# Attention outputs moved by DMA instead of transposes, context tiles turned beside the value projection, and the two maxima pairs of a step placed apart

## The chip, the cores and the metric

The kernel runs on one core of one Trainium2 chip, in one launch for the whole batch. The metric is the device time in microseconds; the kernel before took 1804.34 us (median of three runs, 1802.04 to 1804.83).

## The reference, cut to what matters

Eight batch elements, each with 512 query rows and 1601 context rows of 256 columns, go through cross attention (16 heads of 16 columns) and then a feed-forward part whose four linear layers' operands are rounded to FP4 in blocks of 16.

```python
q = split(layernorm(x) @ Wq.T + bq); k = split(ctx @ Wk.T + bk); v = split(ctx @ Wv.T + bv)
attn = softmax(einsum('bhqd,bhkd->bhqk', q, k) / 4)
x = x + merge(einsum('bhqk,bhkd->bhqd', attn, v)) @ Wo.T + bo
h = silu(fp4(layernorm(x)) @ fp4(w_gate).T) * (fp4(layernorm(x)) @ fp4(w_up).T)
out = x + fp4(h) @ fp4(w_down).T
```

## The kernel before, in words

**Steps.** A batch element's attention is 52 steps: 4 groups of 4 heads, and in each group 13 tiles of the context (`KROWS`: twelve of 128 rows and one of 65). In step n PE makes the scores of two heads (`scores(n, 0)`, line 685, tile `st`), does a large job, makes the scores of the other two heads (`scores(n, 1)`, the same two banks of `st`), makes products for the maxima (`pair_products`, line 699, tile `mx`), does a small job, and multiplies the probabilities of the step before with the values (`weighted`, line 714, tile `pvb`). ACT takes the exponentials (`exps`, line 870) out of `st` into `prob`; the second pair of scores can go to a bank of `st` only when the first pair's exponential has been read out of it.

**Maxima.** The row maxima that the softmax subtracts are made ahead, from bf16 leading parts of q and k, 104 products per batch element, two in each step. A product fills two banks of `mx`, with two heads at once on two halves of the array's rows (48 rows from row 0 and 48 from row 64). DVE reduces each (line 941, 1024 columns) and frees its banks. Before the change both products of a step stand behind the second pair of scores, and in the first batch element a third one behind line 714 for ten steps.

**Jobs.** All other PE work is spread over the steps by a table written by hand: `SLOTS[n]` names the jobs of side 0 (the large one) and of side 1 (the small one), each as (kind, index, part). A part says whose batch element it is: "att" the current one, "early" the next one's projections, "late" the feed-forward of the one before, "once" the weights' rounding, "next" one further ahead. Kinds: `ctxT` turns the context rows (two tiles of 128 per job, line 559), `xnT` the normed queries and `xqT` the FP4 rows (line 521), `k`, `q`, `v` the projections (lines 582, 570, 589), `gate`, `up`, `down0`, `down` the feed-forward (lines 632, 644, 652), `hqT` its rounded middle (line 640), `nm` the maxima (line 597). All of them use one PSUM bank, `misc`, so a job waits until ACT or DVE has taken the one before. `DVE_EXTRA` and `POOL_WORK` are the same kind of table for work on DVE and POOL, placed behind the maxima and the takings of a step.

**Attention's way out, before.** A group's output and the sums of its weights (a 17th column of ones in `vv`) stand in `pvb` as columns by queries. ACT copies them to `pvs` (line 876), PE turns them (`pvT`, line 601, four transposes), ACT copies values and sums apart (lines 811, 812), DVE divides (`group_divided`, lines 999 and 1002), and two jobs `attT` turn the finished rows back (line 521) for the output projection `o` (line 611).

**Iterations.** The program is unrolled: "pre" (projections of the first element), "first", six "loop", "last", and "tail" (the last element's feed-forward). SP issues nearly all DMAs in one order written by hand (`body` of the sync block), each behind its waits: keys and queries go out to memory in three bf16 parts and come back stacked for the scores.

## Time and profile before

| | |
|---|---|
| runs, median of 3 | 1804.34 us |
| the profiled execution | 1801.16 us, span 1799.4 us, granted clock 0.984 |
| PE busy | 1687.2 us, 94% |
| DVE, ACT, POOL busy | 1398.6, 1155.4, 528.4 us (78%, 64%, 29%) |
| chain that ended last | PE 74%, DVE 15%, ACT 7% |
| one batch element in the loop | 210.3 us, 52 steps |

The slices of the page show PE at 9 tenths of every slice from the second to the 36th, with the clock at full; before that the first projections wait for memory, and after it the tail's feed-forward alternates between PE and DVE. PE's matmuls are pipelined: the time that one takes from the engine is the distance between its start and the next one's start, and not its listed length.

### The profile page before, as it was taken

What the parts mean: (1) busy time and instruction counts of PE and PEld (TensorE: products, weight loads), DVE (VectorE), ACT (ScalarE), POOL (GpSimd) and SP (SyncE); (2) the same over time, 40 slices, a digit from 0 to 9 for tenths busy, and PEclk for the clock granted to TensorE, in tenths of its full rate; (3) what the DMA queues carried; (4) which work ended last, traced back from release to release, by engine and by line L of the source; (5) the groups of instructions that cost most, each with busy time, mean ns of one, the idle gap of its engine ahead of it and who ended that gap; (6) DMA issues with size and microseconds to landing.
All of it is one profiled execution on the core that took longest, in us unless ns stands there. A gap on an engine that the chain in (4) does not pass through costs nothing.

```text
span 1799.4 us, 26659 instructions
## 1 busy us (share of the span) xinstructions
PE 1687.2 (94%) x9600; PEld 658.4 (37%) x9600; DVE 1398.6 (78%) x1969; ACT 1155.4 (64%) x2335; POOL 528.4 (29%) x409
## 2 busy tenths in 40 slices
PE   3799789999999999999999999999999999989978
PEld 2332124333343343433443333433334334423425
DVE  6777887888868887788878888688877887688538
ACT  2366567776667666776667766676667766666651
POOL 4316340442107320152204421073201622012213
PEclk8899999999999999999999999999999999999989
DMA  6643432142323322043221423243220422300000
GB/s 147 151 77 92 90 77 37 47 116 38 55 37 96 91 49 50 13 110 73 55 52 44 118 40 55 37 96 90 50 48 12 108 40 43 52 1 1 7 18 12
DMA packets 98031, 109.09 MB, mean 61 GB/s; under 512 B 18788, under 2 KB 83308, under 8 KB 97900
## 3 DMA queue, kind: packets, MB, share of 16 engines
q1 hardware_dynamic: 93344, 103.26, 27.1%
q10 hardware_dynamic: 4556, 4.13, 1.1%
q8 instruction: 76, 1.25, 0.3%
q14 instruction: 55, 0.45, 0.1%
HBM read 76.78 MB, written 30.16 MB: 59 GB/s over the span
## 4 chain that ended last, share of the span: by engine, by line
PE 74%; DVE 15%; ACT 7%; issue 3%; DMA 1%; ACTq 0%; POOL 0%; SPq 0%; DVEq 0%; POOLq 0%
PE pvb L714 19%; PE st L685 18%; PE mx L699 9%; PE misc L632 7%; DVE cmx L941 6%; PE misc L582 5%; ACT prob L870 4%; PE misc L589 4%; PE misc L644 2%; PE misc L652 2%; PE misc L521 1%; PE misc L640 1%; PE misc L611 1%; PE misc L570 1%; PE misc L559 1%
## 5 line engine op out<-in xcount | busy, mean ns | idle before, releaser
L870 ACT ACTIVATE prob<-st 128x512 f32<-128x512 f32 x1630 | 887.6, 599 | 419.9 <-PE st L685 418.2
L941 DVE TENSOR_REDUCE cmx<-mx 128x2 f32<-128x1024 f32 x768 | 905.3, 1219 | 215.4 <-PE mx L699 211.7
L685 PE MATMUL st<-qstack,kstack 112*128 112x512 bf16 x1630 | 520.6, 386 | 32.6 <-ACT prob L870 20.0
L714 PE MATMUL pvb<-prob,vv 128*17 128x512 f32 (+1 forms) x3328 | 440.7, 601 | 0.6 <-ACT prob L870 0.6
L685 PEld LDWEIGHTS st<-qstack,kstack 112*128 112x128 bf16 x1630 | 128.4, 98 | 554.9 <-issue 315.7
L699 PE MATMUL mx<-kstack,qstack 48*128 48x512 bf16 (+1 forms) x2048 | 253.3, 336 | 32.8 <-DMA qstack<-scr_q 16.3
L1202 POOL TENSOR_TENSOR cin<-cin 128x400 f32<-128x400 f32 (+1 forms) x60 | 55.3, 922 | 418.6 <-ACT cin L798 418.6
L1235 POOL TENSOR_TENSOR ht<-ht,rh 128x704 f32<-128x704 f32 x29 | 40.2, 1385 | 425.0 <-DVE rh L917 425.0
L632 PE MATMUL misc<-wguT,rowsT 128*128 128x352 f32 x456 | 154.9, 462 | 0.0
L699 PEld LDWEIGHTS mx<-kstack,qstack 48*128 48x128 bf16 x2048 | 58.0, 94 | 195.7 <-issue 147.2
L632 PEld LDWEIGHTS misc<-wguT,rowsT 128*128 128x128 f32 x456 | 87.1, 191 | 41.4 <-issue 1.0
L589 PE MATMUL misc<-wv,ctxT 128*128 128x256 f32 (+1 forms) x392 | 101.9, 382 | 0.0
L714 PEld LDWEIGHTS pvb<-prob,vv 128*17 128x17 f32 (+1 forms) x3328 | 55.1, 95 | 117.4 <-issue 98.1
L582 PE MATMUL misc<-ctxT,wk 128*128 128x400 f32 (+1 forms) x240 | 91.9, 505 | 0.0
L589 PEld LDWEIGHTS misc<-wv,ctxT 128*128 128x128 f32 (+1 forms) x392 | 73.0, 187 | 21.2 <-issue 0.7
L1239 POOL TENSOR_TENSOR ht<-ht,mt 128x704 f32<-128x704 f32 x30 | 50.4, 1679 | 64.5 <-DVE mt L1120 64.5
L1206 POOL TENSOR_TENSOR cin<-cin 128x400 bf16<-128x400 f32 (+1 forms) x60 | 60.7, 1011 | 4.7
L1215 POOL TENSOR_TENSOR x<-x,bob 128x1024 f32<-128x1024 f32 x8 | 18.9, 2362 | 145.2 <-DMA x<-x 145.2
L975 DVE SCALAR_TENSOR_TENSOR ht<-misc,ht 128x352 f32<-128x352 f32 x57 | 29.7, 521 | 39.4 <-PE misc L632 39.4
L943 DVE TENSOR_REDUCE cmx<-mx 128x8 f32<-128x520 f32 x64 | 44.5, 695 | 19.3 <-PE mx L699 18.3
L1204 POOL TENSOR_TENSOR cin<-cin,one 128x400 bf16<-128x400 f32 (+1 forms) x60 | 56.4, 940 | 4.7
L582 PEld LDWEIGHTS misc<-ctxT,wk 128*128 128x128 f32 x240 | 46.1, 193 | 24.2 <-issue 1.7
(201 smaller groups left out, 1593.3 us busy)
## 6 DMA issues: line engine op xcount, KB each, us to landing
kstack<-scr_k SPq DMA_DIRECT2D x384, 100.1 KB, 4.3
scr_k<-cin SPq DMA_DIRECT2D x48, 300.0 KB, 3.2
qstack<-scr_q SPq DMA_DIRECT2D x372, 32.0 KB, 1.9
cin<-ctx_in SPq DMA_DIRECT2D x8, 1280.0 KB, 6.6
scr_q<-qp SPq DMA_DIRECT2D x15, 384.0 KB, 5.4
scr_k<-cin SPq DMA_DIRECT2D x16, 300.8 KB, 4.4
xn<-x SPq DMA_DIRECT2D x8, 512.0 KB, 3.9
x<-x SPq DMA_DIRECT2D x8, 512.0 KB, 3.8
```

Of the source, the lines that this page charges most:

```text
L582: last = mm(o[:, 0:w], wk[:, h, m * 128:(m + 1) * 128], ctxT[:, h, COFF[n]:COFF[n] + w], start=(h == 0), stop=(h == NC2 - 1))
L589: last = mm(o[0:w, 0:E], ctxT[:, h, KOFF[j]:KOFF[j] + w], wv[:, h, :], start=(h == 0), stop=(h == NC2 - 1))
L632: last = mm(o[:, 0:IH], rowsT[:, h, t * 128:(t + 1) * 128], wguT[:, h, first:first + IH], start=(h == 0), stop=(h == NC2 - 1))
L685: mm(score_bank(it, n, pair, h)[0:KROWS[kt], :], kstack[:, hd, KOFF[kt]:KOFF[kt] + KROWS[kt]], qstack[:, hd, :], start=True, stop=True).th ...
L699: last = mm(mx[:, q % 2, par, at:at + w], qstack[r0:r0 + LEAD, hd, t * 128:(t + 1) * 128], kstack[r0:r0 + LEAD, hd, k0:k0 + w], start=True ...
L714: last = mm(pvb[32 * h:32 * h + D + 1, :], vv[0:w, kt, HG * g + h, :], prob[0:w, n % 2, h, :], start=(kt == 0), stop=(kt == NKT - 1))
L870: activate(prob[0:KROWS[kt], n % 2, 2 * pair + h, :], score_bank(it, n, pair, h)[0:KROWS[kt], :], ACT.Exp, scale=SCALE).then_inc(exp_done[ ...
L941: v.tensor_reduce(cmx[:, g % 2, h0:h0 + 2, at:at + 1], products, op=ALU.max, axis=AX.X).then_inc(max_free, 1)
L1202: g_.tensor_tensor(whole, whole, parts[:, 0, :], ALU.subtract).then_inc(step, 1)
L1204: g_.tensor_tensor(parts[:, 1, :], whole, one[:, 0:1].to_broadcast([128, whole.shape[-1]]), ALU.mult).then_inc(step, 1)
L1206: g_.tensor_tensor(parts[:, 2, :], whole, parts[:, 1, :], ALU.subtract).then_inc(done, 1)
L1239: g_.tensor_tensor(y, y, m, ALU.add).then_inc(h_step, 1)
```

## The change

Four things change together. **One:** the order within a step. The first product for the maxima stands directly behind the first pair of scores, ahead of the large job, and the second one stays behind the second pair of scores; DVE's list has the first reduction ahead of the taking of the large job. **Two:** the attention's way out. `vv` holds, per pair of heads, 16 value columns, 16 ones, 16 value columns, and a head multiplies 32 neighbouring ones of these, so its sum of weights comes out 16 times. SP moves values and sums from `pvs` to `att` and `sums` by eight DMAs of 16 rows by 512 columns a group; DVE divides in eight pieces of 128 columns; `pvT`, `attT` and their copies go. **Three:** a context tile is turned right behind each `v` job (its "guest", two transposes into the other half of `misc`), instead of in seven jobs of two tiles. **Four:** jobs move up into the free slots; `xnT` uses the storage of `mt`, and some waits guard that.

```diff
 SLOTS = {
-    0: ([("v", 8, "att")], [("ctxT", 0, "early")]),
-    1: ([("v", 9, "att")], [("pvT", 3, "late")]),
-    2: ([("v", 10, "att")], [("attT", 0, "late")]),
-    3: ([("v", 11, "att")], [("attT", 1, "late")]),
-    4: ([("v", 12, "att")], [("ctxT", 1, "early")]),
-    5: ([("o", 0, "late")], [("ctxT", 2, "early")]),
-    6: ([("o", 1, "late")], [("ctxT", 3, "early")]),
-    7: ([("ctxT", 4, "early")], [("ctxT", 5, "early")]),
-    8: ([("ctxT", 6, "early")], [("xnT", 0, "early")]),
-    9: ([("k", 0, "early")], [("xnT", 1, "early")]),
+    0: ([("v", 8, "att")], [("ctx2", 0, "once")]),
...
+    4: ([("v", 12, "att")], []),
+    5: ([("o", 0, "late")], []),
+    6: ([("o", 1, "late")], []),
+    7: ([("xnT", 0, "early")], []),
+    8: ([("xnT", 1, "early")], []),
+    9: ([("k", 0, "early")], []),
...
-    18: ([("pvT", 0, "att")], [("xqT", 0, "late")]),
-    19: ([("k", 7, "early")], [("xqT", 1, "late")]),
+    18: ([("k", 7, "early")], []),
+    19: ([("xqT", 0, "late")], [("xqT", 1, "late")]),
...
-    31: ([("gate", 5, "late")], [("pvT", 1, "att")]),
+    31: ([("gate", 5, "late")], []),
...
-    41: ([("down", 2, "late")], [("pvT", 2, "att")]),
+    41: ([("down", 2, "late")], []),
...
 DVE_EXTRA = {
...
+    2: [("late", "values", 4)], 3: [("late", "values", 5)], 4: [("late", "values", 6)], 5: [("late", "values", 7), ("late", "stats", 0)], 6: [("late", "stats", 1)],
...
+    29: [("att", "values", 0)], 30: [("att", "values", 1)], 32: [("att", "values", 2)], 33: [("late", "hscale", 2)], 34: [("late", "hpower", 2)], 35: [("att", "nm", 3)], 36: [("att", "values", 3)], 39: [("late", "hscale", 3)], 40: [("late", "hpower", 3)],
...
+            def values_in(it, g, part):
+
+                sp.wait_ge(pvs_done, it.count(part, NG, g + 1))
+                c, s = divmod(g, 2)
...
+                for h in range(HG):
+                    row = HALF * s + D * h
+                    values, weights = 2 * D * h + D * (h % 2), 2 * D * h + D * (1 - h % 2)
+                    sp.dma_start(att[row:row + D, c, :], pvs[values:values + D, :]).then_inc(values_row[g], 16)
+                    if it.kind != "tail":
+                        sp.dma_start(sums[row:row + D, :], pvs[weights:weights + D, :]).then_inc(values_row[g], 16)
...
                     elif kind == "o":
+                        pe.wait_ge(att_ready, c(NC2 * QT, QT + 2 * j + 2))
...
+                def context_tile(job):
+                    _, j, part = job
...
+                    w, o = KROWS[j], job_bank(it, job)
+                    for h in range(NC2):
+                        last = turn(o[:, h * 128:h * 128 + w], ctx_rows[0:w, j, h * 128:(h + 1) * 128], ident[0:w, 0:w])
+                    last.then_inc(full["ctxT"], 1)
...
-                        last = mm(pvb[32 * h:32 * h + D + 1, :], vv[0:w, kt, HG * g + h, :], prob[0:w, n % 2, h, :], start=(kt == 0), stop=(kt == NKT - 1))
+                        last = mm(pvb[2 * D * h:2 * D * (h + 1), :], vv[0:w, kt, (HG * g + h) // 2, D * (h % 2):D * (h % 2 + 2)], prob[0:w, n % 2, h, :], start=(kt == 0), stop=(kt == NKT - 1))
...
                     if has_att:
                         scores(n, 0)
+                    products = maxima(it, n)
+                    for job in products[:1]:
+                        pair_products(job)
                     for job in jobs(it, n, 0):
                         shared(job)
                     if has_att:
                         scores(n, 1)
-                    products = maxima(it, n)
-                    for job in products[:2]:
+                    for job in products[1:2]:
                         pair_products(job)
...
+                def values_divided(part, n):
+
+                    c, t = divmod(n, QT)
+                    cols = slice(128 * t, 128 * (t + 1))
+                    if t == 0:
+                        for g in (2 * c, 2 * c + 1):
+                            dve.wait_ge(values_row[g], it.count(part, 128, 128))
+                    v.reciprocal(sums[:, cols], sums[:, cols]).then_inc(rec_ready, 1)
+                    dve.wait_ge(rec_ready, it.count(part, NC2 * QT, n + 1))
+                    v.tensor_tensor(att[:, c, cols], att[:, c, cols], sums[:, cols], ALU.mult).then_inc(att_ready, 1)
...
                 for n in range(STEPS):
+                    todo = maxima(it, n)
+                    for job in todo[:1]:
+                        maximum(job)
                     for job in jobs(it, n, 0):
                         take(job)
...
-                    for job in todo:
+                    for job in todo[1:]:
                         maximum(job)
```

In the built program, PE's list at step 2 of a loop iteration (a `v` job, line 589 before and 652 now) reads as follows, first before:

```order
L685 MATMUL st<-qstack,kstack 128x512 x2
L589 MATMUL misc<-wv,ctxT 128x256 x2
L685 MATMUL st<-qstack,kstack 128x512 x2
L699 MATMUL mx<-kstack,qstack 128x512 x4
L521 MATMUL misc<-ident,att 128x128 x4
L714 MATMUL pvb<-prob,vv 17x512 x4
```

The same step now:

```order
L751 MATMUL st<-qstack,kstack 128x512 x2
L765 MATMUL mx<-kstack,qstack 128x512 x2
L652 MATMUL misc<-wv,ctxT 128x256 x2
L728 MATMUL misc<-ident,cin 128x128 x2
L751 MATMUL st<-qstack,kstack 128x512 x2
L765 MATMUL mx<-kstack,qstack 128x512 x2
L780 MATMUL pvb<-prob,vv 32x512 x4
```

Half of the products for the maxima moved between the first scores and the projection, four transposes of `att` went, and two of a context tile came behind the projection.

DVE's list from step 2 to the two steps with the output projection, now (the pieces of the division are lines 1076 and 1078, the reductions for the maxima line 1014, the takings of `o` line 1039):

```order
L1014 TENSOR_REDUCE cmx<-mx 128x2 x3
L1076 RECIPROCAL sums<-sums 128x128
L1078 TENSOR_TENSOR att<-att,sums 128x128
L1014 TENSOR_REDUCE cmx<-mx 128x2 x2
L1076 RECIPROCAL sums<-sums 128x128
L1078 TENSOR_TENSOR att<-att,sums 128x128
L1014 TENSOR_REDUCE cmx<-mx 128x2 x2
L1076 RECIPROCAL sums<-sums 128x128
L1078 TENSOR_TENSOR att<-att,sums 128x128
L1014 TENSOR_REDUCE cmx<-mx 128x2
L1039 TENSOR_TENSOR x<-misc,x 128x512
L1014 TENSOR_REDUCE cmx<-mx 128x2
```

Before, the same stretch held one division of a group and the reductions:

```order
L941 TENSOR_REDUCE cmx<-mx 128x2
L999 RECIPROCAL rec<-den 128x16
L1002 TENSOR_TENSOR att<-att,rec 128x4x64
L941 TENSOR_REDUCE cmx<-mx 128x2 x6
L966 TENSOR_TENSOR x<-misc,x 128x512
```

The division became four wide pieces that end one step ahead of the second `o` job, and the taking of `o` stands between two reductions instead of ahead of both.

## Rows read from the trace of the kernel before

**Rows 1.** The page, part 1: busy time and share of each engine.
```profile
PE 1687.2 (94%) x9600; PEld 658.4 (37%) x9600; DVE 1398.6 (78%) x1969; ACT 1155.4 (64%) x2335; POOL 528.4 (29%) x409
```

**Rows 2.** Busy by stretch: one batch element of the loop (stretch, length, busy by engine).
```profile
508.40:718.70 210.30, 206.59 (x1199) 80.94 (x1200) 168.07 (x237) 143.62 (x290) 61.85 (x49) 1.00 0.29 63
```

**Rows 3.** Timeline of PE, a step with a feed-forward job (start, length, engine, line).
```profile
599.76 1.05 PE L714 MATMUL pvb<-prob,vv 128*17 128x512 f32 x8
600.75 0.60 PE L685 MATMUL st<-qstack,kstack 112*128 112x512 bf16 x2
601.19 1.35 PE L632 MATMUL misc<-wguT,rowsT 128*128 128x352 f32 x4
602.37 0.60 PE L685 MATMUL st<-qstack,kstack 112*128 112x512 bf16 x2
602.90 0.61 PE L699 MATMUL mx<-kstack,qstack 48*128 48x512 bf16 x4
603.44 1.05 PE L714 MATMUL pvb<-prob,vv 128*17 128x512 f32 x8
```

**Rows 4.** Timeline of PE in "pre": one product for the maxima, then a projection.
```profile
66.47 0.39 PE L699 MATMUL mx<-kstack,qstack 48*128 48x512 bf16 x2 [0.49 <-DVE cmx L941]
66.79 1.13 PE L589 MATMUL st<-wv,ctxT 128*128 128x256 f32 x4
67.86 0.39 PE L699 MATMUL mx<-kstack,qstack 48*128 48x512 bf16 x2
```

**Rows 5.** Timeline of PE, a step with a value projection.
```profile
697.00 1.03 PE L589 MATMUL misc<-wv,ctxT 128*128 128x256 f32 x4
697.87 0.71 PE L685 MATMUL st<-qstack,kstack 112*128 112x512 bf16 x2
698.51 0.60 PE L699 MATMUL mx<-kstack,qstack 48*128 48x512 bf16 x4
```

**Rows 6.** Timeline of PE, four transposes in side 1.
```profile
511.83 0.66 PE L521 MATMUL misc<-ident,att 128*128 128x128 f32 x4
512.42 1.05 PE L714 MATMUL pvb<-prob,vv 128*17 128x512 f32 x8
```

**Rows 7.** Timeline of all engines, a step of the loop with a key projection.
```profile
570.55 0.60 PE L685 MATMUL st<-qstack,kstack 112*128 112x512 bf16 x2
570.75 0.60 ACT L797 ACTIVATE cin<-misc,bqk 128x400 f32<-128x400 f32 x1 [0.65 <-PE misc L582]
571.72 1.09 ACT L870 ACTIVATE prob<-st 128x512 f32<-128x512 f32 x2
```

**Rows 8.** Timeline of PE in "last": a step without jobs, from one L714 to the next.
```profile
1606.14 1.05 PE L714 MATMUL pvb<-prob,vv 128*17 128x512 f32 x8
...
1609.62 1.05 PE L714 MATMUL pvb<-prob,vv 128*17 128x512 f32 x8
```

**Rows 9.** Groups by line and form, DVE (count | busy us, mean ns of one | idle).
```profile
L999 DVE RECIPROCAL rec<-den 128x16 f32<-128x16 f32 x32 | 7.8, 244 | 15.8 <-ACT att L812 15.8
L1046 DVE RECIPROCAL rx<-sx 128x64 f32<-128x64 f32 x7 | 3.9, 553 | 0.2
L977 DVE TENSOR_TENSOR x<-x,misc 128x256 f32<-128x256 f32 x29 | 12.1, 416 | 20.6 <-PE misc L652 19.5
```

**Rows 10.** Issues of SP in the timeline, and the DMA view (KB each, us to landing).
```profile
606.69 5.47 SPq L425 DMA_DIRECT2D qstack<-scr_q  x12
qstack<-scr_q SPq DMA_DIRECT2D x372, 32.0 KB, 1.9
```

**Rows 11.** Timeline: a side-1 job behind a gate job.
```profile
631.14 0.66 PE L601 MATMUL misc<-ident,pvs 128*128 128x128 f32 x4 [0.21 <-DVE ht L970]
```

**Rows 12.** Timeline of the tail: the last group's copy and the first addition of `o`.
```profile
1736.14 0.59 ACT L876 COPY pvs<-pvb 128x512 f32<-128x512 f32 x1 [1.17 <-PE pvb L714]
1741.35 0.69 DVE L966 TENSOR_TENSOR x<-mx,x 128x512 f32<-128x512 f32 x1 [2.62 <-PE mx L611]
```

**Rows 13.** Groups by line and form, PE: the products' idle time and who ended it.
```profile
L699 PE MATMUL mx<-kstack,qstack 48*128 48x512 bf16 x1536 | 244.5, 384 | 31.8 <-DMA qstack<-scr_q 16.3 <-DVE cmx L941 15.0
```

More of the change, by code:

```diff
@@ L123 @@
 PRE_SLOTS = {
-    5: ([("ctxT", j, "early") for j in range(7)], []),
+    5: ([("ctx2", j, "early") for j in range(7)], []),
     8: ([("xnT", j, "early") for j in range(2)], []),
@@ L173 @@
 TAIL_EXTRA = {
-    1: DVE_EXTRA[1], 3: [("late", "half", 0)], 4: [("late", "half", 1)], 6: [("late", "hscale", 0)],
+    1: [("late", "values", p) for p in range(4, 8)], 3: [("late", "half", 0)], 4: [("late", "half", 1)], 6: [("late", "hscale", 0)],
     7: [("late", "hpower", 0), ("late", "hscale", 1), ("late", "hpower", 1)], 9: [("late", "hscale", 2), ("late", "hpower", 2)],
@@ L333, in job_count, with tiles_turned, guest @@
         def job_count(it, job):
-            return it.count(job[2], PER[job[0]], job[1] + 1)
+            kind, j, part = job
+            if kind == "ctx2":
+                return (PAIRS if part == "once" else 0) + j + 1
+            if part == "once":
+                return j + 1
+            if kind == "ctxT":
+                return tiles_turned(it, part, j + 1)
+            return it.count(part, PER[kind], j + 1)
+        def tiles_turned(it, part, k):
+            return (it.batch(part) - 2) * NKT + NKT - 8 + k
+        def guest(it, job):
+            if job[0] != "v" or it.kind == "pre":
+                return None
+            part = {"early": "next", "att": "early"}[job[2]]
+            return ("ctxT", job[1], part) if part in it.parts else None
         def job_bank(it, job):
+            if job[0] == "ctxT":
+                return misc[:, 2 * 128:]
             b = BANKS.bank(it.kind, job)
@@ L537, in shared @@
                         before = BANKS.last("loop", 0)
-                        assert before == BANKS.last("first", 0) and before[2] == "early"
-                        pe.wait_ge(free[before[0]], it.count("att", PER[before[0]], before[1] + 1))
+                        assert before == BANKS.last("first", 0) and before[0] == "v" and before[2] == "early"
+                        pe.wait_ge(free["v"], it.count("att", NKT, before[1] + 1))
+                        if "early" in it.parts:
+                            pe.wait_ge(free["ctxT"], tiles_turned(it, "early", before[1] + 1))
                     elif it.kind == "tail":
@@ L849, in take @@
                         raw_in(j // 2 + 2)
+                    if guest(it, job):
+                        take(guest(it, job))
                 def first_queries():
@@ L873, in group_out @@
                     act.wait_ge(pv_done, it.count(part, STEPS, NKT * (g + 1)))
-                    if g:
-                        act.wait_ge(full["pvT"], it.count(part, NG, g))
+                    need(act, values_row[(g - 1) % NG], it.count(part, 128, 128 if g else 0))
                     copy(pvs[:, :], pvb[:, :]).then_inc(pvs_done, 1)
+                    if it.kind == "tail":
+                        act.wait_ge(pvs_done, it.count(part, NG, NG))
+                        for h in range(HG):
+                            row, weights = HALF + D * h, 2 * D * h + D * (1 - h % 2)
+                            act.dma_start(sums[row:row + D, :], pvs[weights:weights + D, :]).then_inc(values_row[g], 16)
                 has_att, has_late = "att" in it.parts, "late" in it.parts
@@ L1010, in extra @@
                         split_maxima(part, k)
[L1011 to L1012 removed]
+                    elif what == "values":
+                        values_divided(part, k)
                     elif what == "stats":
@@ L1148, in weight_powers @@
                         dve.wait_ge(wq_done, p)
+                    else:
+                        dve.wait_ge(full["q"], it.count("early", 2, 2))
                     w_linked(v.tensor_scalar(m.bitcast(I32), w.bitcast(I32), EXPONENT, None, ALU.bitwise_and))
@@ L1213, in work @@
                         pool.wait_ge(s_x1, c(16, 16))
+                        if it.kind != "tail":
+                            pool.wait_ge(free["v"], it.count("att", NKT, 10))
                         pool.wait_ge(free["bob"], 1)
```

134 lines of the change are left out of this document (71 added, 63 removed).

## The prediction

> **What bounds the kernel now.** I read the page first: PE is busy 94% of the span and DVE 78% [rows 1]. Then the busy times by stretch, where a batch element in the loop takes 210.3 us and PE is busy for 206.6 of them [rows 2]. So the loop is set by PE's list, and a job is worth what it takes from that list. Third, PE's timeline, for prices. The reader should take the distance between neighbouring starts there [rows 3]: the weighted sums of line 714 take 0.99 us, the first two scores 0.44, the gate job 1.18, the second two scores 0.53, two products for the maxima 0.54. That is 3.68 us with nothing left over, and 2.50 of it are in every step.
>
> Two of these are longer than their columns. The two scores are the same matmuls both times, yet take 0.44 ahead of a job and 0.53 ahead of the products. Ahead of the job the next weights are loaded while the scores still stream; ahead of the products, which use the array in two halves of 48 rows, they are not. The same 0.1 us stands between the products and line 714, which uses it in four strips of columns. So a change of how the array is divided costs about 0.1 us in this kernel, each time.
>
> **The step's order.** Before, a step has three such changes: scores to products, products to line 714, line 714 to scores. The change adds two: first scores to first product, and first product to large job. "Pre" shows a lone product ahead of a float32 job [rows 4]: the product takes 0.32 from its start to the job's, and that `v` job takes 1.07 where it takes 0.87 between scores [rows 5]. Of these 0.20 more, 0.10 are its own exit to the next product, which it will not have here, and 0.10 are a first float32 load that nothing covers. A step is then 0.53 + 0.32 + 0.10 + 0.53 + 0.32 + 0.99 = 2.79 us plus its jobs, 0.29 to 0.30 more than 2.50. I take 0.30: 52 steps give **+15.6 us** per batch element. Nothing lies beside this, since PE is what the others wait for.
>
> The Trainium skill, "TensorEngine Tiling (Array Packing)", section "Key Properties", says that changing the tiling mode drains TensorE, without a figure; it speaks against this change, and the 0.53 beside 0.44 agrees with it. The Trainium skill, "TensorE: Matmul & The Clock Gate", section "Step-by-step: what each phase is for", says that weight loads are pulled ahead so that the next tile's weights load during this tile's matmul; by that alone the 0.30 would be nothing, which the same rows contradict wherever the division changes. That outcome is the first rival below.
>
> **What else moves, per batch element of the loop.**
> - Four transposes in side 1 take 0.59 us [rows 6]. Thirteen such jobs go from side 1 (five `ctxT`, three `pvT`, two `attT`, and two `xnT` and one `xqT` that become large jobs): **-7.7**.
> - Thirteen `v` jobs get a guest of two transposes. They stay in the array's full form, so I count half of the 0.43 that four take without the 0.16 around them: 0.21. Against that, the second scores behind a `v` take 0.64 where they take 0.53 elsewhere [rows 3, 5], a wait for the exponentials that the product ahead of the job covers: -0.11. **+1.3**.
> - Three steps have a transpose as the large job (7, 8, 18 before; 7, 8, 19 now). They behave like a step without a job, which takes 3.48 us [rows 8]: the second score needs the bank of the first pair's last exponential. With the product in that wait I get 0.53 + 0.32, then a wait, and 3.25 in all. They gain 0.23 instead of losing 0.30: **-1.6**.
> - Key and query jobs are near a ring through ACT. From the second scores' start, ACT's first copy comes at 0.20, the exponentials at 1.17, and they end at 2.26 [rows 7]. PE wants the second score of the next step, which needs the bank of the last of them, at 0.53 + 0.54 + 0.99 + 0.22 = 2.28 before, and at 0.53 + 0.32 + 0.99 + 0.22 = 2.06 now. So each of the ten steps waits about 0.25, where now it waits nothing to 0.2: **+1.5**.
> - A side-1 job behind a gate waits for DVE to free `misc`, 0.21 us in the case shown [rows 11]. It will come 0.22 earlier and wait that much longer; four steps: **+0.9**.
> - The division. A reciprocal takes 244 ns for 16 columns and 553 for 64 [rows 9], so by the line through both some 0.95 us for 128; the product is under the 416 ns of 256 columns, say 0.28. A piece is 1.25 us, and a step has two reductions, so it fits in the ordinary step. Only piece 7, behind the taking of the first `o` and two reductions, ends about 1.6 us into the step of the second `o`, which PE wants at 0.95: **+0.7**. Lower bound 0, if the reciprocal is as cheap as for 64 columns.
> - PE's waits for late reductions, about 16 us in the whole run [rows 13], should shrink, since a product's banks now have a whole step to come free: about **-1**.
>
> The DMAs: eight per group at 0.47 us of SP's time and 1.9 to land (the nearest row has the same 32 KB) [rows 10]. They are issued in 3.7 us. For group 3, line 714 of its last tile ends with step 0, some 4 us into the new element, and ACT's copy 0.6 later; so the issues begin at 4.7 and all has landed at about 10.4, ahead of DVE's first piece at 12 (behind three steps of 3.9). The keys and queries that SP issues behind them are wanted more than ten steps later, except that `q` and `k` parts go out 4 us later, also with steps to spare. ACT's copies for `pvT` and `attT` go and smaller ones for guests come; ACT is not what ends a step except in the ring above. POOL's splits of k and q move by at most two steps; I cost that at nothing, because what reads them are the stacking DMAs with steps to spare, and if that cover were gone a late split would hold ACT's copy for the key job two later. Wider results of line 714 (32 columns for 17) I cost at nothing, because its strips are loaded together; if each first load were longer by its own share, it could be 0 to 0.1 us a step.
>
> **Sum.** One element: 15.6 - 7.7 + 1.3 - 1.6 + 1.5 + 0.9 + 0.7 - 1.0 = +9.7, say 9.5. Six loops: +57. "First" has no late part: its thirteen `v` steps (+0.4 with the guest) and ten `k` and `q` steps (+0.5) lose some 10, three context jobs gone (-1.8) and half of its twenty empty steps at -0.23 give back about 4: +6. "Last" has maxima only up to step 33: sixteen steps with jobs at +0.30 and the second `o`, its `v` steps at +0.2, against five transposing jobs: +3. The tail: from the copy's start to the first addition of `o` 5.2 us pass [rows 12], or 4.6 from its end. Now come four issues on each of two queues (1.9), a landing (1.9), and four pieces of 1.25 on DVE ahead of that addition: 8.8, so +4. "Pre" has its products alone already: 0. In all +70 on the profiled execution's own 1801.2: 1871. The median of the runs stands 3.2 above that execution, so I forecast **1874 us**, 3.9% slower.
>
> **Rivals.**
> - *The loads are hidden after all* (faster): the products' weights come in while scores or jobs stream, because the lone product asks for one load per half. Then the 15.6 go, and the ring's 1.5: an element gains 7, six of them 42; "first" and "last" come to about -4, the tail keeps +4, and the result is 1762. For it: float32 jobs behind scores show no gap. Against: every change of division in the rows shows one. Chance 0.07.
> - *About half of the price is paid*, because part of the exposed load falls into waits that the steps have anyway: an element costs +2, and the run ends near 1829. For it: the waits for exponentials exist. Against: in the gate step there is none to fall into. Chance 0.12; with a little more cover it is no change at all, 0.03.
> - *The values come late* (slower still): if the landings take as long as those of larger transfers, DVE sits at the first piece with the reductions behind it, and PE's products wait for DVE; decided from about 1.6 us of delay on. A step's length lost in each of seven elements is 31 us: 1905. Against: the queue is empty there. Chance 0.10.
>
> **How the numbers follow.** My own case has 0.68, around 1874. Faster takes the first rival, 0.07; within 0.2% (3.6 us, what a measurement here can tell from no change) 0.03; slower has the rest, 0.90. The range leaves out the first rival, no change, and the ends of the second and third: 1838 to 1902. Its lower end is an element at +5 (0.2 per step for the order), its upper end one at +13 (a little wider line 714, or longer rings).
>
> **What would show it.** Right: a gate step with 0.53 for the first scores, 0.32 for a lone product, about 1.29 for the gate, and 3.98 in all; an element of 219 to 221 us; PE's busy share no lower than now with DVE's higher by some 6 us an element. Wrong: first scores of 0.44 ahead of the product (the loads are hidden), a `k` step under 4.3 (no ring), or DVE idle at line 1076 behind a DMA (late values).

## The result, and the profile after the change

The changed kernel takes 1868.93 us (median of 4 runs, 1868.27 to 1871.24) where the kernel before took 1803.89 beside it (4 runs, 1802.04 to 1804.83): a ratio of 1.0366, with a 95% interval of 1.0352 to 1.0379. It is slower by 65 us; the forecast was 1874, by 70. The profiled execution of the changed kernel took 1868.27 us with a span of 1866.5.

The page, part 1, of the changed kernel, and the busy times of one batch element of its loop (stretch, length, then busy time of PE, PEld, DVE, ACT and POOL):

```profile
PE 1754.2 (94%) x9408; PEld 657.2 (35%) x9408; DVE 1458.8 (78%) x2032; ACT 1133.0 (61%) x2293; POOL 526.9 (28%) x409
```
```profile
519.02:739.26 220.24, 216.31 (x1172) 80.80 (x1171) 175.38 (x244) 140.76 (x288) 61.65 (x50) 1.00 0.31 65
```

PE has 192 matmuls fewer than before [rows 1] and is busy 67 us longer. The element grew by 9.9 us [rows 2], and PE's busy time in it by 9.7, so the growth is time in which the profile shows PE as busy and not as idle. It is no added work (1172 matmuls for 1199), which is why the distances between starts have to be read next. DVE grew by 7.3 and is still idle a fifth of the time.

PE's timeline for a step with a gate job, which answers to [rows 3], with the side-1 job that stands ahead of it:

```profile
604.49 0.28 PE L660 MATMUL misc<-ident,nmx 128*16 128x128 f32 x1 [0.42 <-DVE ht L1043]
604.70 1.06 PE L780 MATMUL pvb<-prob,vv 128*32 128x512 f32 x8
605.70 0.60 PE L751 MATMUL st<-qstack,kstack 112*128 112x512 bf16 x2
606.23 0.39 PE L765 MATMUL mx<-kstack,qstack 48*128 48x512 bf16 x2
606.55 1.45 PE L687 MATMUL misc<-wguT,rowsT 128*128 128x352 f32 x4
607.84 0.60 PE L751 MATMUL st<-qstack,kstack 112*128 112x512 bf16 x2
608.37 0.39 PE L765 MATMUL mx<-kstack,qstack 48*128 48x512 bf16 x2
608.69 0.64 PE L780 MATMUL pvb<-prob,vv 128*32 128x512 f32 x4
```

Again the distance between starts is what counts. First scores 0.53 (0.44 before), lone product 0.32, gate 1.29 (1.18 before), second scores 0.53, second product 0.32 (the pair took 0.54 before), weighted sums 1.00: 3.99 us for 3.68. The side-1 job in the first line waits 0.42 us for DVE where it waited 0.21 [rows 11].

A step with a key job, PE and ACT, which answers to [rows 7]:

```profile
586.83 0.60 PE L751 MATMUL st<-qstack,kstack 112*128 112x512 bf16 x2
587.03 0.59 ACT L873 ACTIVATE cin<-misc,bqk 128x400 f32<-128x400 f32 x1 [1.18 <-PE misc L645]
587.99 2.25 ACT L939 ACTIVATE prob<-st 128x512 f32<-128x512 f32 x4
588.67 0.85 PE L751 MATMUL st<-qstack,kstack 112*128 112x512 bf16 x2
589.46 0.39 PE L765 MATMUL mx<-kstack,qstack 48*128 48x512 bf16 x2
```

From 588.67 the two scores take 0.79 instead of 0.53: the second of them waits until ACT has finished the exponentials, which stand behind two copies of the key job.

The step of the second `o` job, the division on DVE (two groups; count, busy us, mean ns, idle) and its transfers (KB each, us to landing):

```profile
536.62 0.39 PE L765 MATMUL mx<-kstack,qstack 48*128 48x512 bf16 x2
537.75 1.97 PE L666 MATMUL misc<-wo,att 128*128 128x256 f32 x8 [0.74 <-DVE att L1078]
```
```profile
L1076 DVE RECIPROCAL sums<-sums 128x128 f32<-128x128 f32 x64 | 60.2, 941 | 18.1 <-DMA sums<-pvs 18.1
L1078 DVE TENSOR_TENSOR att<-att,sums 128x128 f32<-128x128 f32 x64 | 21.5, 336 | 2.2
```
```profile
att<-pvs SPq DMA_DIRECT2D x128, 32.0 KB, 1.9
```

The 18.1 us behind a DMA are 17.4 in the tail and less than 1 in all seven elements, so the values do not come late. The tail, which answers to [rows 12], and its granted clock (stretch, length, busy by engine, clock, DMA):

```profile
1797.35 0.58 ACT L944 COPY pvs<-pvb 128x512 f32<-128x512 f32 x1 [1.19 <-PE pvb L780]
1797.97 2.70 ACTq L950 DMA_DIRECT2D sums<-pvs  x4
1802.16 0.95 DVE L1076 RECIPROCAL sums<-sums 128x128 f32<-128x128 f32 x1 [17.41 <-DMA sums<-pvs]
1804.78 3.68 PE L666 MATMUL misc<-wo,att 128*128 128x256 f32 x8 [7.49 <-DVE att L1078]
1808.29 1.89 PE L666 MATMUL st<-wo,att 128*128 128x256 f32 x8
1808.50 0.69 DVE L1039 TENSOR_TENSOR x<-misc,x 128x512 f32<-128x512 f32 x1 [1.49 <-PE misc L666]
```
```profile
1804.70:1808.50 3.80, 3.73 (x9) 3.06 (x10) 2.24 (x5) 0.00 (x0) 0.00 (x0) 0.53 0.00 0
```

From the copy's start to the first addition of `o` 11.15 us pass, where 5.2 passed before. The `o` job takes 3.5 us there to the next one's start and 1.81 in the loop; the granted clock of that stretch is 0.53, which is almost all of it at 1.2 GHz, after PE had been idle for 7.5 us.

Stage by stage, from the first weighted sums of one element to those of the next: "pre" 86.3 to 90.0, "first" 211.6 to 208.8, the six loops 1260.0 to 1319.3, "last" 177.1 to 178.0, tail 64.4 to 70.3. That is +3.7, -2.8, +59.3, +0.9 and +5.9, in all 67.1, the whole difference of the spans.

### The profile page after: what moved, and what is told of

It is laid out like the page before. It is cut to its first block, busy times and chain, and to the rows that moved or that the text cites. A ratio compares the mean times of both kernels' runs of the same rounds, so it can differ in the third digit from the quotient of the medians.

```text
span 1866.5 us, 26605 instructions
## 1 busy us (share of the span) xinstructions
PE 1754.2 (94%) x9408; PEld 657.2 (35%) x9408; DVE 1458.8 (78%) x2032; ACT 1133.0 (61%) x2293; POOL 526.9 (28%) x409
## 4 chain that ended last, share of the span: by engine, by line
PE 76%; DVE 10%; ACT 9%; issue 2%; DMA 1%; ACTq 0%; POOL 0%; SPq 0%; DVEq 0%; POOLq 0%
PE st L751 17%; PE pvb L780 17%; PE mx L765 11%; PE misc L687 8%; PE misc L652 5%; ACT prob L939 5%; PE misc L645 5%; DVE cmx L1014 4%; PE misc L699 2%; PE misc L707 2%; PE misc L666 2%; PE misc L695 1%; PE misc L631 1%; ACT cin L873 1%; ACT cin L874 1%
## 5 line engine op out<-in xcount | busy, mean ns | idle before, releaser
L1014 DVE TENSOR_REDUCE cmx<-mx 128x2 f32<-128x1024 f32 x768 | 934.2, 1223 | 271.3 <-PE mx L765 263.7
L751 PE MATMUL st<-qstack,kstack 112*128 112x512 bf16 x1630 | 509.7, 384 | 18.9 <-ACT prob L939 5.5
L780 PE MATMUL pvb<-prob,vv 128*32 128x512 f32 (+1 forms) x3328 | 445.0, 607 | 0.6 <-ACT prob L939 0.6
L765 PE MATMUL mx<-kstack,qstack 48*128 48x512 bf16 (+1 forms) x2048 | 318.8, 339 | 31.8 <-DMA qstack<-scr_q 18.0
L765 PEld LDWEIGHTS mx<-kstack,qstack 48*128 48x128 bf16 x2048 | 84.8, 93 | 363.0 <-issue 182.7
L687 PE MATMUL misc<-wguT,rowsT 128*128 128x352 f32 x456 | 164.8, 484 | 0.0
L780 PEld LDWEIGHTS pvb<-prob,vv 128*32 128x32 f32 (+1 forms) x3328 | 65.7, 108 | 86.9 <-issue 79.0
L878 ACT COPY vv<-misc 128x256 f32<-128x256 f32 (+1 forms) x98 | 36.4, 372 | 67.6 <-PE misc L652 62.6
L873 ACT ACTIVATE cin<-misc,bqk 128x400 f32<-128x400 f32 (+1 forms) x60 | 35.7, 595 | 65.2 <-PE misc L645 63.1
L1076 DVE RECIPROCAL sums<-sums 128x128 f32<-128x128 f32 x64 | 60.2, 941 | 18.1 <-DMA sums<-pvs 18.1
```

Of the source, the lines that this page charges most:

```text
L687: last = mm(o[:, 0:IH], rowsT[:, h, t * 128:(t + 1) * 128], wguT[:, h, first:first + IH], start=(h == 0), stop=(h == NC2 - 1))
L751: mm(score_bank(it, n, pair, h)[0:KROWS[kt], :], kstack[:, hd, KOFF[kt]:KOFF[kt] + KROWS[kt]], qstack[:, hd, :], start=True, stop=True).th ...
L765: last = mm(mx[:, q % 2, par, at:at + w], qstack[r0:r0 + LEAD, hd, t * 128:(t + 1) * 128], kstack[r0:r0 + LEAD, hd, k0:k0 + w], start=True ...
L780: last = mm(pvb[2 * D * h:2 * D * (h + 1), :], vv[0:w, kt, (HG * g + h) // 2, D * (h % 2):D * (h % 2 + 2)], prob[0:w, n % 2, h, :], start= ...
L1014: v.tensor_reduce(cmx[:, g % 2, h0:h0 + 2, at:at + 1], products, op=ALU.max, axis=AX.X).then_inc(max_free, 1)
L1076: v.reciprocal(sums[:, cols], sums[:, cols]).then_inc(rec_ready, 1)
```

## The experiments

The theory: the order of a step costs 0.30 us wherever a float32 job follows the product (0.10 for each of two more changes of how the array is divided, 0.10 for a float32 weight load that nothing covers), and the new layout gives time back. The rivals: the layout is what costs, or both do; or the price is not in the changes of division but in the lone product. Below, "element" is the mean of the six loops, from each run's own trace; each ratio is to the kernel before, run beside it.

### The old order in the new layout

```diff
-                    products = maxima(it, n)
-                    for job in products[:1]:
-                        pair_products(job)
                     for job in jobs(it, n, 0):
                         shared(job)
                     if has_att:
                         scores(n, 1)
-                    for job in products[1:2]:
+                    products = maxima(it, n)
+                    for job in products[:2]:
```

and on DVE both reductions again behind the taking of the large job.

> The changed layout with the old order of a step: both products for the maxima behind the second scores, and both reductions behind the taking of the large job's result. Theory (the order costs about 0.30 us per step, the layout gives time back): the loop's element falls from 220.2 us by 15.6 for the order, 1.5 for the ring of key and query jobs and 0.9 for waits behind gate jobs, and gives back 1.6 in the steps with a transposing job, 1.4 in the second scores behind v jobs and 1.0 for late reductions, so it ends at about 206; pre falls back by 3.7 us; in all about 1770 us, faster than the kernel before. Gate step 3.68 us with 0.44 for its first scores. Rival, the layout is what costs (divisions on DVE, 56 new transfers, guests): no change in PE's steps beyond those with a job moved, 1860 to 1870 us. Rival, both carry half: about 1820 us.

Measured: 1789.74 us (ratio 0.9923, 0.9908 to 0.9938). A gate step is back at 3.69, and the element at 207.5. So the layout alone is faster than the kernel before, by 0.8%, and the rival falls. The 20 us above the expectation come from two waits that are longer with the old order: the step of the second `o` job takes 6.45 us in the element shown and up to 8.08 in others (5.32 in the changed kernel), and step 37 5.62 (5.07). With both moved away, further below, the six loops are 26 us shorter. DVE and PE in the step of the second `o` job:

```profile
517.27 2.36 DVE L1012 TENSOR_REDUCE cmx<-mx 128x2 f32<-128x1024 f32 x2
519.54 0.94 DVE L1074 RECIPROCAL sums<-sums 128x128 f32<-128x128 f32 x1
520.52 0.29 DVE L1076 TENSOR_TENSOR att<-att,sums 128x128 f32<-128x128 f32 x1
520.95 1.97 PE L666 MATMUL misc<-wo,att 128*128 128x256 f32 x8 [1.97 <-DVE att L1076]
```

The last piece's division stands behind two reductions whose products come late in the step; with a product ahead, the first reduction is done earlier, and the wait is 0.74.

### The new order in the old layout

The same two moves, made in the kernel before; nothing else.

> The old layout with the new order of a step: the first product for the maxima ahead of the large job, its reduction ahead of the taking of that job's result. Theory (the order costs 0.30 us per step wherever a float32 job follows the product): the loop's element rises from 210.3 us by 15.6 for the order, 1.5 for the ring, 0.9 behind gate jobs, less 1.6 in transposing steps, 1.4 behind v jobs and 1.0 for late reductions, to about 224; with about 4 each for first, last and pre, about 1895 us (1885 to 1905). Rival, the order is harmless and the layout is the cost: 1800 to 1808 us. Rival, half each: about 1840 us.

Measured: 1896.34 us (ratio 1.0517, 1.0501 to 1.0532), as expected. The element is 224.8, 14.7 above the kernel before. So the order costs 88 us in the loops, and the new layout takes 29 of them back (1348.5 for six loops here, 1319.3 in the changed kernel).

### The first product behind the large job

```diff
-                    for job in products[:1]:
-                        pair_products(job)
                     for job in jobs(it, n, 0):
                         shared(job)
+                    for job in products[:1]:
+                        pair_products(job)
                     if has_att:
                         scores(n, 1)
```

with the reductions on DVE behind the taking.

> The changed kernel, but the first product stands behind the large job and ahead of the second scores. The array's division still changes five times in a step, but the large float32 job now follows scores, so its first load is covered; what is uncovered is the second scores' bfloat16 load. The large job also ends 0.4 us earlier against the second scores, so ACT's copy for a key or query job starts earlier. Theory (each change 0.10 us, and another 0.10 for the uncovered float32 load): gate step 3.88 us instead of 3.99, first scores 0.44, no ring wait in key and query steps; the loop's element 213 to 216 us, in all 1825 to 1845 us. Rival, a lone product costs the same wherever it stands: gate step 3.98, about 1865 us. Rival, all of the price is the product ahead of a float32 job: gate step 3.68 to 3.75, below 1800 us.

Measured: 1811.19 us (ratio 1.0043, 1.0028 to 1.0058). The step is as the theory had it:

```profile
589.80 0.60 PE L751 MATMUL st<-qstack,kstack 112*128 112x512 bf16 x2
590.24 1.35 PE L687 MATMUL misc<-wguT,rowsT 128*128 128x352 f32 x4
591.52 0.39 PE L765 MATMUL mx<-kstack,qstack 48*128 48x512 bf16 x2
591.84 0.61 PE L751 MATMUL st<-qstack,kstack 112*128 112x512 bf16 x2
592.38 0.39 PE L765 MATMUL mx<-kstack,qstack 48*128 48x512 bf16 x2
592.70 1.06 PE L780 MATMUL pvb<-prob,vv 128*32 128x512 f32 x8
```

First scores 0.44, gate 1.28 (its exit into a product), 0.32, 0.54, 0.32, 1.00: 3.90, two changes more than 3.69 and no uncovered load. The total is below the range, as the element is (211.9 for 213 to 216): key steps lost their ring, and some lost nothing at all against the old order (4.07 in step 16 with either).

### Both products ahead of the large job

```diff
-                    for job in products[:1]:
+                    for job in products[:2]:
...
-                    for job in products[1:2]:
-                        pair_products(job)
```

and both reductions ahead of the taking.

> The changed kernel with both products for the maxima ahead of the large job (and both reductions ahead of the taking of its result): no lone product, four changes of the array's division in a step instead of five, but a float32 job still stands behind a product. The runs so far gave the gate step 3.68 us with three changes and 3.90 with five changes and the float32 load covered. Theory (0.10 us per change, and 0.10 more for a float32 load that nothing covers): 3.68 + 0.10 + 0.10 = 3.88 us. Rival, the number of changes alone counts: 3.78 to 3.79. Rival, a lone product is what costs: 3.68. Key steps have the ring's wait as in the changed kernel or longer, and jobs of side 1 behind a gate wait for its taking, some 1 us later; so the whole stays near the changed kernel, 1850 to 1890 us by the theory, and the step is what tells the cases apart.

Measured: 1902.76 us (ratio 1.0558, 1.0542 to 1.0573), 13 above the range.

```profile
629.97 0.60 PE L751 MATMUL st<-qstack,kstack 112*128 112x512 bf16 x2
630.51 0.61 PE L765 MATMUL mx<-kstack,qstack 48*128 48x512 bf16 x4
631.04 1.45 PE L687 MATMUL misc<-wguT,rowsT 128*128 128x352 f32 x4
632.33 0.60 PE L751 MATMUL st<-qstack,kstack 112*128 112x512 bf16 x2
632.86 1.07 PE L780 MATMUL pvb<-prob,vv 128*32 128x512 f32 x8
```

0.54 + 0.53 + 1.29 + 0.53 + 1.00 is 3.89, so a single change more than before costs 0.21 when a float32 job follows it. The gate job itself is as long behind a pair as behind a lone product (1.29); the lone product is not what costs, and the uncovered load is. PE's weight loads show it. The first load of the gate job, in the kernel before, the changed kernel, the one with the product behind the job, and this one:

```profile
600.97 1.00 PEld L632 LDWEIGHTS misc<-wguT,rowsT 128*128 128x128 f32 x4
606.55 0.89 PEld L687 LDWEIGHTS misc<-wguT,rowsT 128*128 128x128 f32 x4 [0.23 <-issue]
590.03 1.00 PEld L687 LDWEIGHTS misc<-wguT,rowsT 128*128 128x128 f32 x4
631.04 0.89 PEld L687 LDWEIGHTS misc<-wguT,rowsT 128*128 128x128 f32 x4 [0.43 <-issue]
```

Behind scores it starts 0.21 to 0.22 us ahead of the gate's first matmul (601.19 and 590.24); behind a product it starts with it (606.55 and 631.04). What the 0.10 of a change of division itself is, stays open. Across a change the next load starts only with its matmul, for products and scores too, and a bfloat16 load is listed with 0.10 us and a float32 one with 0.19; a single rule, that the whole first load behind a change is uncovered, gives the same prices. No run here tells the two readings apart. The whole is slower still because the taking of a job's result now stands behind two reductions: step 32, whose transposes in side 1 wait for that bank, takes 5.40 where the changed kernel takes 4.58.

### The product ahead only where no float32 product follows

```diff
+                def ahead(it, n):
+                    return int("att" in it.parts and all(j[0] in ("xnT", "xqT", "wT") for j in jobs(it, n, 0)))
...
-                    for job in products[:1]:
+                    early = ahead(it, n)
+                    for job in products[:early]:
```

the same on DVE, and the `o` jobs at steps 6 and 7 (`xnT` 0 at 5), the statistics one step later too.

> The changed layout; the first product stands ahead only in steps whose large job is missing or transposes and whose element has maxima in this very kernel stage, behind the second scores elsewhere; and the two o jobs (with the statistics behind them) go one step later, behind the transposes of xn, so that the division of piece 7 has a step more. Theory: as the old order in the new layout (about 1770 us), less 0.23 us in each of three transposing steps of six loops and some 20 empty steps of the first element (about 8 us), and less the 0.8 us that the second o job waits for DVE, seven times (about 6 us): about 1757 us (1745 to 1770). Rival, a lone product costs 0.3 us in an empty step too: about 1775 us. Rival, the order is not what costs: 1855 to 1870 us.

Measured: 1755.52 us (ratio 0.9736, 0.9720 to 0.9752): faster than both kernels. Step 37 still took 5.63:

```profile
633.71 0.67 PE L769 MATMUL mx<-kstack,qstack 48*128 48x512 bf16 x4
633.85 0.93 DVE L1081 RECIPROCAL sums<-sums 128x128 f32<-128x128 f32 x1
634.82 0.29 DVE L1083 TENSOR_TENSOR att<-att,sums 128x128 f32<-128x128 f32 x1
635.02 0.52 DVE L1048 SCALAR_TENSOR_TENSOR ht<-xn,misc 128x352 f32<-128x352 f32 x1
635.60 0.66 PE L699 MATMUL misc<-ident,ht 128*128 128x128 f32 x4 [1.23 <-DVE ht L1048]
```

The transposes at the end wait for the bank that DVE's line 1048 frees, and that stands behind a piece of the division.

### Piece 3 of the division two steps later, and the same with no and with every product ahead

```diff
-    35: [("att", "nm", 3)], 36: [("att", "values", 3)], 39:
+    35: [("att", "nm", 3)], 38: [("att", "values", 3)], 39:
```

in the kernel above; in the second and third, `ahead` returns 0 or 1 everywhere.

> As the kernel with the product ahead only in empty or transposing steps, with DVE's division of piece 3 at step 38 instead of 36. There step 37 took 5.63 us, because its transposes of side 1 waited 1.35 us for DVE to free the bank, and DVE was busy with step 35's maxima of a group (2.0 us) and piece 3 (1.2 us). Theory (DVE's list is full for these two steps alone): step 37 falls to about 4.3 us and nothing is late at step 38, seven elements by 1.3 us: 9 us less, about 1746 us. Rival, the wait moves to step 39 or 40, where the scales of the gate's blocks follow: no change, 1753 to 1757 us.

> As the kernel with piece 3 at step 38 (and the o jobs one step later), but with both products behind the second scores in every step: the old order in the new layout without its two collisions on DVE. Theory: the empty and transposing steps lose what the product ahead gave them, 0.2 us in some 20 steps of the first element and in three steps of each loop: 6 to 8 us more than with it, about 1753 us. Rival, the order is worth nothing there: the same within 3 us.

> As the one before, but with the first product ahead of the large job in every step: the order of the changed kernel, in a layout without its collisions on DVE (the o jobs one step later, piece 3 at step 38). Theory: the changed kernel (1869 us) less 0.8 us for the second o job in seven elements and up to 0.5 for step 37, so 1858 to 1864 us; and against the order with none ahead, 0.30 in each of some 42 steps with a float32 job, the ring's 0.2 in ten, less 0.2 in the transposing ones: about 105 us. Rival, the changed kernel's loss was mostly collisions on DVE that came with the layout: 1800 to 1840 us.

Measured: 1749.69 us (0.9705, 0.9689 to 0.9721), 1763.65 (0.9784, 0.9770 to 0.9799) and 1863.86 (1.0342, 1.0327 to 1.0357). Step 37 fell to 4.56, not to 4.3 (4.56 is about what it took before the change, 4.54), so the gain was 6 and not 9. The price of the order with the collisions on DVE out of the way is 100 us, for 105 expected; one element of each, none ahead and then all ahead:

```profile
499.00:702.20 203.20, 200.58 (x1172) 80.15 (x1170) 171.75 (x245) 140.90 (x287) 61.51 (x50) 1.00 0.33 70
```
```profile
520.00:739.50 219.50, 216.30 (x1176) 80.81 (x1178) 175.79 (x244) 140.86 (x288) 61.69 (x50) 1.00 0.31 65
```

16.3 us of length, 15.7 of them PE's busy time, with the same jobs in both. Step by step the difference is 0.25 to 0.33 us in 34 of the 52 steps, 0.38 to 0.73 in fifteen, most of which have a wait for ACT or DVE on top, and -0.22 in two transposing ones. Step 19 alone takes 1.10 less with every product ahead: without, ACT's copies for the key job of step 18 start 1.5 us behind the second scores and not 0.2, for a reason that the trace does not show. The collision at the second `o` job was worth 5 us of the changed kernel's loss (1868.9 to 1863.9; 0.8 in each loop of the traces), as its 0.74 in seven elements would have it; step 37 keeps its 5.07 there, so piece 3 was not what it waited for in that order. Without any product ahead the run is 14 us slower than with those in empty and transposing steps, twice the expectation. The traces differ by 10.7: 3 in the loops (0.5 each), 7 in "first", 2 in "last", less 1 in "pre" and the tail; the rest lies between the runs.

### Work for PE in the tail

```diff
                     elif kind == "o":
+                        if it.kind == "tail" and j == 0:
+                            for _ in range(15):
+                                mm(o[:, 0:512], ident[:, :], wguT[:, 0, 0:512], start=True, stop=True)
                         pe.wait_ge(att_ready, c(NC2 * QT, QT + 2 * j + 2))
```

in the fastest kernel and in the changed one, then both with 8 in place of 15.

> The fastest kernel so far (product ahead only in empty or transposing steps, o one step later, piece 3 at step 38), and in the tail, between the last weighted sums and the first o job, PE computes 15 float32 products of 128 x 512 that nothing reads, into the bank that the o job then overwrites. There PE had been idle for 7.5 us, the granted clock was 0.50 in the stretch of the first o job, and the two o jobs took 3.55 and 2.79 us against 1.80 in the loop. Theory (the idle time is what lowers the clock): 1.80 and 1.9 us, so 2.5 us less in the tail, about 1747 us. Rival, the o jobs are slow because the pieces of the division come one by one: no change, 1748 to 1751 us.

> The changed kernel, and the same 15 products in the tail that nothing reads, between the last weighted sums and the first o job. Theory (of the tail's 5.9 us over the kernel before, 1.8 are the first o job at a granted clock of 0.53): that job takes 1.8 to 2.0 us instead of 3.5, and the tail is 1.7 us shorter; about 1867 us, which the trace shows better than the times. Rival, the job waits for the pieces: no change in the tail's 70.3 us.

> The fastest kernel with 8 instead of 15 such products in the tail: each took 0.86 us, so 15 of them filled 13.1 us and stood 5 us in front of the o job, which then ran at a granted clock of 1.00 in 1.73 us. Eight fill 6.9 us of the 7.5. Theory (idle time lowers the clock): both o jobs at 1.7 to 1.9 us as with 15, and the first starts when the division lets it; the tail is 2.5 us shorter than the fastest kernel's, a ratio to the kernel before of 0.9690 where that one had 0.9705. Rival, the clock was kept by the products standing directly ahead of the job: a gap of 0.6 us lowers it again, no change.

> The changed kernel with 8 such products in the tail. Theory: first o job 1.7 to 1.9 us where it took 3.5, the tail 68.5 us instead of 70.3, and the whole 1867 us; the ratio 1.0355 where the changed kernel had 1.0366, which the interval cannot tell, so the tail's rows decide. Rival as in the other run: no change.

With 15 the products took 13.1 us, since one takes 0.86 and not the 0.43 that I had reckoned with, and both tails grew by some 3.5 us (to 74.3 and 73.9). The whole runs, 1755.22 us (0.9733, 0.9716 to 0.9750) and 1873.03 (1.0390, 1.0371 to 1.0409), stand above those without the products, though the intervals overlap. But the first `o` job then took 1.73 us to the next one's start, at a granted clock of 1.00. With 8 (the changed kernel's tail):

```profile
1796.65 7.13 PE L664 MATMUL misc<-wguT,ident 128*128 128x512 f32 x16
1804.13 1.99 PE L669 MATMUL misc<-wo,att 128*128 128x256 f32 x8 [0.35 <-DVE att L1081]
1806.37 0.68 DVE L1042 TENSOR_TENSOR x<-misc,x 128x512 f32<-128x512 f32 x1
1806.60 1.96 PE L669 MATMUL st<-wo,att 128*128 128x256 f32 x8 [0.47 <-DVE att L1081]
```
```profile
1804.20:1806.00 1.80, 1.80 (x8) 1.37 (x8) 1.77 (x3) 0.00 (x0) 0.00 (x0) 1.00 0.00 0
```

The clock stays at 2.4 GHz over the gap of 0.35, so the idle time before is what had lowered it. The tail falls from 70.3 to 69.3 us, not to 68.5: the second `o` job now waits for DVE's last piece. In the fastest kernel it falls from 70.8 to 68.4, as forecast, but the second `o` job starts 1.1 to 1.2 us earlier in both, and tails with the same instructions differ by about as much, so 1.1 is what these rows show. Whole runs, 1748.14 us (0.9702, 0.9688 to 0.9716) and 1866.75 (1.0359, 1.0344 to 1.0374), cannot be told from those without the products.

## Why the prediction was right, point by point

**The step's order.** Right in its mechanism and its size. The gate step has 3.99 for 3.98, each part as forecast, and four arrangements of the same instructions took what a price of 0.10 per change of division and 0.10 per uncovered float32 load gives: 3.68 with three changes, 3.90 with five and the load covered, 3.89 with four and the load uncovered, 3.99 with five and the load uncovered. The Trainium skill, "TensorEngine Tiling (Array Packing)", section "Key Properties", has the drain at a change of tiling mode without a figure; the rows agree that a change costs, and give the figure for this kernel.

One sign that I had named for being wrong did show: a `k` step under 4.3. Step 9 takes 4.16, because the ring's wait falls into the step behind a key or query job, and step 9 has none ahead of it; the other seven `k` steps take 4.31 to 5.10.

The first rival (loads hidden) and the second (half the price) are out by the same rows, since first scores of 0.53 and 3.99 a step leave no room for them; the third (late values) by DVE's idle time behind a DMA, under 1 us in the elements.

**The sum of one element.** Forecast +9.7, taken as 9.5; measured +9.9. Split by the run with the order alone: order +14.7, where my terms for it give 14.0 (15.6 + 1.5 + 0.9 - 1.6 - 1.0, and 13 times 0.11 for second scores behind `v`); layout -4.9, where the rest of my terms give -4.3 (-7.7, 13 guests of 0.21, and 0.7). Term by term: the ring is 0.26 for 0.25; the wait behind a gate 0.42 for 0.21 + 0.22; the wait of the second `o` 0.74 for 0.7; the reciprocal 941 ns for 950, its multiplication 336 for 280 (292 in the median; the eight of 64 that meet work of POOL take 0.49 to 1.67 us); landings 1.9 for 1.9. Only the late reductions fell short: their idle time goes from 15.0 [rows 13] to 12.8 us in the whole run, 0.3 an element and not 1.

The two parts don't simply add, though. With the old order the new layout gains only 2.5 an element, because the division then collides with DVE's reductions, and the new order, of itself a loss, hides these waits. With the collisions moved away, the old order leaves the new layout an element of 203.1, 7 below the kernel before.

**"First": +6 forecast, -2.8 measured.** The step that failed is the count of what it loses and gives back. The new order alone made "first" 3.3 slower there, and the layout 6.1 faster. I had let the layout give back only three context jobs, and had left out the transposing `pvT` jobs, which "first" has as well: steps 31 and 41 take 3.84 each with the order alone and 3.27 in the changed kernel. Most lies elsewhere: 5.5 of the 6.1 are in steps 20 to 34, which took 66.5 us before, 65.3 with the order alone and 59.8 now. There PE waits for reductions (`cmx`) that stand on DVE behind the rounding of weights, and part of what follows runs at the low clock. The waits for reductions, PE's busy time and the granted clock are 11.7 us, 51.9 us and 0.89 with the order alone, and 8.6, 49.2 and 0.94 in the changed kernel. One such wait, in the latter:

```profile
176.85 2.46 DVE L1065 TENSOR_TENSOR nmr<-nmf,nmp 16x128 f32<-16x128 f32 x1
182.76 0.39 PE L765 MATMUL mx<-kstack,qstack 48*128 48x512 bf16 x2 [3.75 <-DVE cmx L1014]
```

The subtraction takes 0.28 us the sixteen times that it finds POOL idle, and 0.82 to 2.46 the sixteen times that POOL's work overlaps it, as the rounding does here. The weighted sums behind the wait are listed with 1.93 us, those ahead of it with 1.07. My sum had neither these waits nor the clock, so that the stretch gained is luck. Some of it changes from one execution to the next: the fastest kernel's list, traced three times (twice with other tails), takes 60.6, 63.3 and 60.5 there, at a granted clock of 0.94, 0.89 and 0.94; the changed kernel's takes 59.8, 60.5 and 60.5. The kernel before does not have PE at 9 tenths all along either: in slices 5 and 6 of its page, which lie in "first", it has 7 and 8.

**"Last": +3 forecast, +0.9 measured.** Its steps 9 to 19 have no key or query job and are nearly all empty, and there the product ahead gains: they fall from 40.0 to 36.9 us, and with the order alone to 37.6. I had counted the empty steps of "first" and not those of "last".

**Tail: +4 forecast, +5.9 measured.** The chain was right: from the copy's end to the first addition of `o` I had 8.8 us, and the changed kernel takes 10.57. With PE kept busy it takes 8.99 (1797.38 to 1806.37). So of the 1.8 us that it took beyond my 8.8, 1.6 are the missing term, the `o` job at the low clock. The Trainium skill, "TensorE: Matmul & The Clock Gate", section "What's actually happening", says that a hardware block sets the array's clock by how busy it has been recently, with 1.2 GHz when idle; the granted clock of 0.53 and of 1.00 in the two tails agrees, and I had not applied it to the 7.5 us of idle time that my own sum put there. All eight kernels with the new layout and no such products have a tail of 69.7 to 70.8 us, both with the old one 64.2 to 64.4.

**"Pre": 0 forecast, +3.7 measured.** Not settled. The kernels with the old order there take 86.3 to 90.2 us to the first weighted sums, those with the new one 87.5 to 90.0. The fastest kernel, which has the old order there, takes 87.3, and 90.2 and 88.7 with the products in its tail, though nothing in "pre" differs between the three; so the scatter is nearly as large as the +3.7, and an effect of the order is not shown. PE's idle time behind the transfer of stacked queries there goes from 16.3 [rows 13] to 18.0 us; I had set nothing down for it.

So the errors are -8.8, -2.1, +1.9, +3.7 and +2.3 (loops): 67.1 for 70. The loops were forecast; outside them the sum is better than its parts by luck, since the misses cancel in part.

## What to carry to other kernels

Before moving a matmul, look at how its neighbours divide the array: here each change of division costs 0.10 us, a float32 weight load behind one another 0.10, and both vanish in the busy time of PE, where only the distance between starts shows them. Move it into a step in which PE waits anyway, and it is a gain (0.2 us in an empty step); into one with a float32 job, a loss of 0.3. And undo each half of a two-part change by itself: the layout here was worth 29 us in the loops beside the order that hid it, and the two together, with the order kept to the empty steps, gave 3% where the change lost 3.7%.

## What was not expected of the hardware

A job of 1.8 us took 3.5 after PE had been idle for 7.5 us, at a granted clock of 0.53; 7.1 us of products that nothing reads kept it at 1.00, over a last gap of 0.35 us. A float32 product of 128 x 512 takes 0.86 us, in two passes of 0.43 in the trace. And weighted sums of 32 columns, for 17 before, cost 1.00 us a step for 0.99 [rows 3]: the widened strips are nearly free. A subtraction of 16 x 128 on DVE took 0.28 us by itself and up to 2.46 while POOL was at work.
